# A first expert mixture over all tokens of nine experts against one over fifteen single-expert tiles of sent rows

## The reference, cut to what matters

```python
def _L0_ffn_ref(x, w_router, W1, b1, W2, b2, Ws1, bs1, Ws2, bs2):
    probs = jax.nn.softmax(jnp.einsum('btd,ed->bte', x, w_router), axis=-1)
    vals, idx = jax.lax.top_k(probs, TOP_K)                      # TOP_K = 2 of 8
    gates = jnp.sum(jax.nn.one_hot(idx, N_EXPERTS, dtype=x.dtype) * vals[..., None], axis=-2)
    hs = jax.nn.gelu(jnp.einsum('btd,fd->btf', x, Ws1) + bs1)    # shared expert
    acc = jnp.einsum('btf,df->btd', hs, Ws2) + bs2
    h = jax.nn.gelu(jnp.einsum('btd,efd->btef', x, W1) + b1)     # 128 -> 512
    y = jnp.einsum('btef,edf->bted', h, W2) + b2                 # 512 -> 128
    return SCALE * (acc + jnp.einsum('bted,bte->btd', y, gates))

def _L1_attn_ref(x, W_qkv, b_qkv, W_out, b_out, w_sur, b_sur, threshold):
    qkv = x @ W_qkv + b_qkv                                      # 16 heads of 8
    tq, sq = _expmap0_split(q); tk, sk = _expmap0_split(k)       # cosh and sinh of a norm
    dist = jnp.arccosh(jnp.maximum(tq tk - sq sk, 1.0 + 1e-07))
    attn = softmax(where(causal, -dist ** 2 / sqrt(D), -inf)) * spike_mask
...
x = x + _L0_ffn_ref(_layernorm(x), ...)
x = x + _L1_attn_ref(_layernorm(x), ...)
```

## Time and profile before

| | |
|---|---|
| median of three runs | 1193.46 us (1186.05, 1193.46, 1195.53) |
| the profiled execution's own time | 1186.87 us |
| its span | 1185.6 us |
| PE busy | 976.0 us, 82% of the span |
| DVE / ACT / POOL busy | 782.7 / 589.5 / 245.0 us |
| mean granted PE clock | 0.902 |
| bytes moved by DMA | 62.49 MB, mean 53 GB/s |
| on the chain that ended last | PE 57%, DVE 28%, ACT 5%, POOL 4% |

### The profile page before, as it was taken

How to read it: one execution, slowest core, us unless ns; L and a number is a source line. 1 busy time by engine, 2 the same in 40 slices (tenths; PEclk the granted TensorE clock), 3 DMA queues, 4 the chain that set the end, 5 groups by cost and what they waited for, 6 DMA issues and landing times.

```text
span 1185.6 us, 20975 instructions
## 1 busy us (share of the span) xinstructions
PE 976.0 (82%) x8169; PEld 552.0 (47%) x8169; DVE 782.7 (66%) x1990; ACT 589.5 (50%) x1019; POOL 245.0 (21%) x321
## 2 busy tenths in 40 slices
PE   6777779998999975767658999999578688689999
PEld 4233334444676752545433334566223233357667
DVE  7786888821326479878678963867787877664512
ACT  2556546674335347778627785223045456343342
POOL 2843220000000235967420000001120001100000
PEclk9898979998999985878877999999568889989999
DMA  8324250000000310491125007101003000100000
GB/s 315 103 71 94 63 188 2 3 5 1 1 1 1 107 37 1 143 182 54 47 68 185 2 3 107 43 1 44 11 28 134 2 1 2 36 1 1 10 1 10
DMA packets 35894, 62.49 MB, mean 53 GB/s; under 512 B 5235, under 2 KB 25668, under 8 KB 34196
## 3 DMA queue, kind: packets, MB, share of 16 engines
q1 hardware_dynamic: 33828, 58.64, 17.5%
q10 hardware_dynamic: 1968, 2.51, 0.8%
HBM read 43.04 MB, written 16.65 MB: 50 GB/s over the span
## 4 chain that ended last, share of the span: by engine, by line
PE 57%; DVE 28%; ACT 5%; POOL 4%; issue 3%; DMA 2%; SPq 1%; ACTq 0%; POOLq 0%; DVEq 0%
PE ps_s L970 10%; PE ps_e L960 10%; PE ps_v L759 7%; DVE mx L1999 6%; PE ps_e L649 4%; PE ps_e L1065 2%; DVE mx L1991 2%; PE ps_s L1052 2%; DVE ps_s L1973 2%; ACT work L1495 2%; PE ps_e L664 2%; DVE xn L1943 2%; PE ps_s L679 2%; DVE stats L1925 1%; DVE work L2532 1%
## 5 line engine op out<-in xcount | busy, mean ns | idle before, releaser
L1495 ACT ACTIVATE work<-ps_e 128x512 f32<-128x512 f32 x406 | 223.1, 597 | 110.5 <-PE ps_e L649 105.5
L2772 POOL TENSOR_TENSOR rstd<-rstd,halves 128x2 f32<-128x2 f32 x52 | 36.7, 706 | 657.4 <-DVE rstd L1930 657.0
L1999 DVE TENSOR_REDUCE mx<-ps_s 128x2 f32<-128x1024 f32 x128 | 153.6, 1221 | 21.0 <-PE ps_s L679 18.8
L1602 ACT ACTIVATE work<-ps_s,keep 128x512 f32<-128x512 f32 x136 | 93.0, 687 | 139.2 <-PE ps_s L970 136.1
L759 PE MATMUL ps_v<-work,vaug 128*32 128x256 f32 x1536 | 128.0, 408 | 5.0 <-ACT work L1483 4.9
L649 PE MATMUL ps_e<-q_stack,ctx_stack 52*128 52x256 bf16 (+1 forms) x684 | 121.7, 291 | 9.2 <-DMA q_stack<-mT 3.3
L960 PEld LDWEIGHTS ps_e<-ffn_w,work 128*128 128x128 f32 x960 | 117.2, 195 | 21.3 <-issue 19.6
L679 PE MATMUL ps_s<-ctx_stack,q_stack 49*128 49x512 bf16 (+1 forms) x296 | 91.6, 450 | 40.7 <-DVE mx L1999 30.7
L2198 DVE SCALAR_TENSOR_TENSOR x<-ps_e,gates,x 128x128 f32<-128x128 f32 x128 | 38.9, 346 | 124.8 <-PE ps_e L960 119.1
L970 PE MATMUL ps_s<-xnT,ffn_w 128*128 128x512 f32 x240 | 117.6, 614 | 3.6 <-ACT work L1602 3.6
L960 PE MATMUL ps_e<-ffn_w,work 128*128 128x128 f32 x960 | 119.3, 279 | 0.8 <-DVE x L2188 0.8
(11 more groups left out here) (412 smaller groups left out, 1965.9 us busy)
## 6 DMA issues: line engine op xcount, KB each, us to landing
q_stack<-q_scr SPq DMA_DIRECT2D x32, 192.0 KB
ffn_w<-in_L0f_w SPq DMA_DIRECT2D x1, 4608.0 KB, 17.5
ffn_w<-in_L1f_w SPq DMA_DIRECT2D x1, 3456.0 KB, 13.0
q_scr<-parts SPq DMA_DIRECT2D x16, 192.0 KB, 2.1
c_scr<-ffn_w SPq DMA_DIRECT2D x12, 256.0 KB, 7.6
kx_scr<-ffn_w SPq DMA_DIRECT2D x12, 256.0 KB, 3.9
ctx_stack<-kx_scr SPq DMA_DIRECT2D x2, 1536.0 KB
ctx_stack<-c_scr SPq DMA_DIRECT2D x2, 1536.0 KB
```

The costliest lines, as they stand in the source:

```text
L1495: act.activation(pt[:, parity, :, :].rearrange("p k q -> p (k q)"), bank[exp_bank(use, h, parity)], ACT.Exp).then_inc(exped, 1)
L1602: act.activation(hid_unit(st, u)[:, j, :], bank[f"h{n % 2}"], ACT.Gelu_apprx_tanh, bias=b1).then_inc(HIDS[st], 1)
L1999: m = dve.tensor_reduce(mx[:, b, :, pair, part], ps_s[i][:], AX, ALU.max, negate=True)
```

## The change

The mixture's eight routed experts run only over the rows that are sent to them.

- After the router of a half, DVE works out with a few small PE products (`rank`, `destinations`) at which row of a buffer each token's two copies go, so that every tile of 128 rows belongs to one expert, and which expert owns each of the `TILES` = 15 tiles.
- POOL sends the 1024 rows of a half by eight indirect DMAs to DRAM (`scatter`), SP brings the 15 tiles back in one transfer (`fetch_sent`, 960 KB), and PE transposes them (`turn_sent`).
- SP reads the 15 expert numbers into registers (`owners`) and fetches for every tile that expert's weights (128 x 1028 numbers, 514 KB) into a ring of `RING` = 4 places. The fetch for tile i waits until the down products of tile i-4 are done.
- PE does for each tile four up and four down products of 128 x 128 by 128 x 128, two tiles ahead with the ups. ACT does four GELUs of 128 x 128 for each and copies every four tiles' results out of PSUM. SP stores them, and POOL gathers each token's two rows back by eight indirect DMAs a half (`gather`). DVE adds them times the gates (`combine`).
- The shared expert stays dense. Of the products in the last slots of `X0` four are left where there were twelve.
- `EARLY_A1` = `TILES`, so all 36 steps of `l1_early` stand behind the last tile on PE and ACT, and on DVE ahead of `combine(2)` and `combine(3)`. On POOL `gather(1)` stands behind the splitting of batch 1.
- The single transfer of 4608 KB is gone.

```diff
+TILES = 2 * B * S // 2 // P + NE - 1
+RING = 4
+TILE_W = 2 * FH + FJ
+BLOCKS0 = -(-TILES // 4)
+UP_USE = {use: n for n, use in enumerate(
...
+RANK0 = 71
+RANK1 = 3
+GATES0 = 7
+EARLY_A1 = TILES
...
+        def turn_sent(g, q):
+            name = ("v", "m")[q % 2]
+            claim(name)
+            if q == 0:
+                pe.wait_ge(*after(x_there, 16 * (g + 1)))
+            for i in range(4 * q, min(4 * q + 4, TILES)):
+                m = pe.transpose(bank[name][:, i % 4 * P:(i % 4 + 1) * P], xg[:, i, :], ident)
+            m.then_inc(turned_x_ps[0], 1)
+            free[name] = after(turned_x, BLOCKS0 * g + q + 1)
+
...
+        def tile_up(g, i):
+            n, at = UP_USE["tile", g, i], g * TILES + i
+            name, w = f"h{n % 2}", tile_ring[at % RING]
+            claim(name)
+            pe.wait_ge(*after(tile_there[at % RING], 16 * (at // RING + 1)))
+            if i % 4 == 0:
+                pe.wait_ge(*after(turned_x, BLOCKS0 * g + i // 4 + 1))
+            for j in range(FJ):
+                m = pe.matmul(bank[name][:, j * P:(j + 1) * P], w[:, j * P:(j + 1) * P], xgT[:, i, :],
+                              start=True, stop=True)
+            m.then_inc(up_ps, 1)
+            free[name] = (hidden, n + 1)
+
+        def tile_down(g, i):
+            at = g * TILES + i
+            name, w, hid = f"e{i // 4 % 2}", tile_ring[at % RING], tile_hid[at % RING]
+            if i % 4 == 0:
+                claim(name)
+            pe.wait_ge(hidden, UP_USE["tile", g, i] + 1)
+            for j in range(FJ):
+                m = pe.matmul(bank[name][:, i % 4 * P:(i % 4 + 1) * P], hid[:, j, :], w[:, FH + j * E:FH + (j + 1) * E],
+                              start=(j == 0), stop=(j == FJ - 1))
+            m.then_inc(tile_ps[0], 1)
+            free[name] = after(evacuated, BLOCKS0 * g + i // 4 + 1)
+
...
+            shared_down(0)
+            shared_down(1)
+            for q in range(BLOCKS0):
+                turn_sent(0, q)
+            for g in range(2):
+                tile_up(g, 0)
+                tile_up(g, 1)
+                for i in range(TILES):
+                    if i + 2 < TILES:
+                        tile_up(g, i + 2)
+                    tile_down(g, i)
+                    if g == 0 and i == RANK1:
+                        rank(1)
+                    if g == 0 and i == GATES0:
+                        turn_gates("L0f", NE + 1, 1, ROUTE_AT["L0f"] + 1, "v")
+                        gated_bias("L0f", 0, NE + 1, 1, "m")
+                    if g == 1 and i >= EARLY_A1:
+                        l1_early(i - EARLY_A1)
+                if g == 0:
+                    for j in range(FJ):
+                        shared_up(1, j)
+                    for q in range(BLOCKS0):
+                        turn_sent(1, q)
+                    shared_down(2)
+                    shared_down(3)
+            for q in range(TILES - EARLY_A1, 36):
+                l1_early(q)
...
+        def tile_gelu(g, i):
+            n, at = UP_USE["tile", g, i], g * TILES + i
+            w, hid = tile_ring[at % RING], tile_hid[at % RING]
+            if at >= RING:
+                act.wait_ge(*after(tile_ps, at - RING + 1))
+            act.wait_ge(up_ps, n + 1)
+            for j in range(FJ):
+                m = act.activation(hid[:, j, :], bank[f"h{n % 2}"][:, j * P:(j + 1) * P], ACT.Gelu_apprx_tanh,
+                                   bias=w[:, 2 * FH + j:2 * FH + j + 1])
+            m.then_inc(hidden, 1)
+
+        def evacuate(g, k):
+            last = min(4 * k + 4, TILES)
+            n = (last - 4 * k) * P
+            if g == 1 and k == 0:
+                act.wait_ge(*after(y_stored, 16 * BLOCKS0))
+            act.wait_ge(*after(tile_ps, g * TILES + last))
+            act.activation(y_tile[:, k, 0:n], bank[f"e{k % 2}"][:, 0:n], ACT.Copy).then_inc(evacuated[0], 1)
 
...
+            for g in range(2):
+                tile_gelu(g, 0)
+                tile_gelu(g, 1)
+                for i in range(TILES):
+                    if i + 2 < TILES:
+                        tile_gelu(g, i + 2)
+                    if i % 4 == 3 or i == TILES - 1:
+                        evacuate(g, i // 4)
+                    if g == 1 and i >= EARLY_A1:
+                        l1_early(i - EARLY_A1)
+                if g == 0:
+                    for j in range(FJ):
+                        shared_gelu(1, j)
+            for q in range(TILES - EARLY_A1, 36):
+                l1_early(q)
...
+        def combine(b):
+            g = b // 2
+            dve.wait_ge(*after(y_gathered, 128 * (g + 1)))
+            dve.wait_ge(down_x, b + 1)
+            for c in range(2):
+                for t in tiles(b):
+                    m = dve.scalar_tensor_tensor(x[:, t, :], y_rows[:, g, c, t % 4, :], top_gates[:, c, t:t + 1],
+                                                 x[:, t, :], ALU.mult, ALU.add)
+                if c == 0:
+                    settle(m)
+            m.then_inc(combined[0], 1)
...
+            shared_add(0)
+            shared_add(1)
+            for q in range(BLOCKS0):
+                turned_sent(0, q)
+            route_rest("L0f", None, 1, slice(4, 8))
+            destinations(1, slice(4, 8))
+            turn_gates("L0f", NE + 1, 1, "v")
+            gated_bias("L0f", 1, "m")
+            for q in range(BLOCKS0):
+                turned_sent(1, q)
+            shared_add(2)
+            shared_add(3)
+            for b in (0, 1):
+                combine(b)
+                statistics(A1, b)
+                normalised(A1, b)
+            for q in range(36):
+                l1_early(q)
+            for b in (2, 3):
+                combine(b)
+                statistics(A1, b)
+                normalised(A1, b)
 
         def l3_piece(g, i):
             kind, e, k = PIECES[i]
...
+        def scatter(g):
+            pool.wait_ge(*after(destined, g + 1))
+            pool.wait_ge(*after(zeroed, 32))
+            if g == 1:
+                pool.wait_ge(*after(x_scattered, 128))
+            for t in range(4):
+                for c in range(2):
+                    pool.indirect_dma_start(
+                        out=x_sent[g][:, :],
+                        out_offset=bass.IndirectOffsetOnAxis(ap=dest_i[:, g, c * 4 + t:c * 4 + t + 1], axis=0),
+                        in_=xn[:, 4 * g + t, :], in_offset=None).then_inc(x_scattered[0], 16)
+
+        def gather(g):
+            pool.wait_ge(*after(y_stored, 16 * BLOCKS0 * (g + 1)))
+            if g == 1:
+                pool.wait_ge(*after(y_gathered, 128))
+            for t in range(4):
+                for c in range(2):
+                    pool.indirect_dma_start(
+                        out=y_rows[:, g, c, t, :], out_offset=None, in_=y_sent[g][:, :],
+                        in_offset=bass.IndirectOffsetOnAxis(ap=dest_i[:, g, c * 4 + t:c * 4 + t + 1], axis=0),
+                    ).then_inc(y_gathered[0], 16)
+
...
             split_keys(A1, 0, map_T, 2)
             split_keys(A1, 1, map_T, 4)
             split_queries(A1, 1, map_T, 3)
+            gather(1)
             l1_added_least(0)
...
-        for b in range(B):
+        for b in range(3):
             root("L0f", b)
+        scatter(0)
+        root("L0f", 3)
+        scatter(1)
+        gather(0)
         l1_attention()
...
+        def fetch_tile(g, i, owner):
+            at = g * TILES + i
+            if at >= RING:
+                sp.wait_ge(*after(tile_ps, at - RING + 1))
+            sp.dma_start(tile_ring[at % RING], d["L0f_tiles"][bass.ds(owner, 1)].rearrange("o p c -> (o p) c")) \
+                .then_inc(tile_there[at % RING][0], 16)
+
+        def owners(g):
+            sp.wait_ge(*after(destined, g + 1))
+            return [sp.value_load(expert_i[0:1, g, i:i + 1], min_val=0, max_val=NE - 1) for i in range(TILES)]
+
+        def fetch_sent(g):
+            sp.wait_ge(*after(x_scattered, 128 * (g + 1)))
+            if g == 1:
+                sp.wait_ge(*after(turned_x_ps, BLOCKS0))
+            sp.dma_start(xg, x_sent[g].rearrange("(i p) f -> p i f", p=P)).then_inc(x_there[0], 16)
+
+        def store_block(g, k):
+            n = min(4 * k + 4, TILES) - 4 * k
+            sp.wait_ge(*after(evacuated, BLOCKS0 * g + k + 1))
+            sp.dma_start(y_sent[g][4 * k * P:(4 * k + n) * P, :].rearrange("(i p) f -> p i f", p=P),
+                         y_tile[:, k, 0:n * P].rearrange("p (i f) -> p i f", i=n)).then_inc(y_stored[0], 16)
+
...
-        sp.dma_start(ffn_w[:, 0:FFN_N], d["L0f_w"][:, :]).then_inc(d_w, 16)
+        sp.dma_start(shared_w, d["L0f_shared"][:, :]).then_inc(d_w, 16)
+        for g in range(2):
+            sp.dma_start(x_sent[g][:, :], d["zeros"][:, :]).then_inc(zeroed[0], 16)
         for b in range(1, B):
             max_rows(X0, b)
+        owner = owners(0)
+        for i in range(RING):
+            fetch_tile(0, i, owner[i])
+        fetch_sent(0)
         sp.wait_ge(exp_ps, 2 * (STEP0[X0] + STEPS[X0]))
```

(19 more changed lines are left out.)

278 lines of the change are left out of this document (176 added, 102 removed).

## The result

The changed kernel takes 1230.28 us (median of 4 runs, 1226.28 to 1233.76) beside 1190.95 for the kernel before in the same session: 1.033 times, 95% interval 1.027 to 1.039. Run once more beside the experiments (e0_again) it gave 1225.19 us, 1.026 times (1.022 to 1.030). Forecast were 1208 and a range of 1188 to 1232. The sign was right; the loss is 39 us where 15 were forecast. The profiles of f1_banks and a4_again are of slower executions than the rest (over 1.5% above the fastest of the same kernel), so only lengths of stages are read from them.

The account below looks back on a forecast made before the run. PE was taken to bound the mixture. Batch 3 normalised at 450.5 against 434.6 gave +16 us, one us came back, +15; on the profiled 1186.9 that is 1202, plus 6.6 for the median 1208 us, range 1188 to 1232.

Parts of the forecast that it names:

- The end of X0: Before the mixture: eight ups removed bring the last batch's transposes some 5 us earlier; first down from 292.25 to 287.
- cover gone, it would cost these 4 us: End of X0: price of the 17 small DVE steps of destinations(0) if DVE were not waiting there.
- The work of the mixture: Shared expert and tiles: PE's 126 us become about 71, 1.78 us a tile; ACT and DVE don't set the pace.
- The ring of four sets the pace: Tile weights: a fetch takes 3.5 us, so two tiles take 5.3 us where PE needs 3.56; a half 38 us.
- First half: Tiles start at 293.5, half over at 333.5; indirect DMAs 1.3 us each, half 1's rows sent by 322, hidden.
- Between the halves: SP's queue: 15 reads of 0.6 us, then 12 us of transfers; second half's tiles start at 354.5, end at 392.5.
- The opening steps: Behind the last tile: 50.5 us to the last near product, 58 to batch 3 normalised, at 450.5 against 434.6.
- The gap did not close: Rival, between the halves: cheap register reads (0.1 us) close the gap, 14 us go, 1194 us; chance 0.20.
- the fetches were not hidden: Rival, tile weights: the fetches are hidden, 10 us go in each half, 1188 us; chance 0.05.
- the indirect DMAs were not 4 us: Rival, POOL's queue: indirect DMAs cost 4 us each, adding 5 us for sent rows and 14 at gather(1), 1227; chance 0.13.
- PE did not fall to its lower clock in the tiles: Rival, tiles: PE falls to 1.2 GHz, two tiles take 7.1 us instead of 5.3, 1239 us; chance 0.10.
- Faster: Whole kernel: faster by more than about 1%, under 1182 us, given 0.06; slower 0.57, same 0.37.

Follow-up runs that it names:

- f1_banks: Changed kernel with near products and roots of the opening steps taking two PSUM banks in turn instead of one: 1240.58 us, 1.036 times the kernel before.
- a4_again: Changed kernel with opening steps 0 to 20 between tiles 2 to 13 of the second half, second run: 1228.53 us, 1.023 times the kernel before.
- a1_again: Changed kernel with bank m freed early by a DVE copy of ranks and counts, second run: 1226.53 us, 1.026 times the kernel before.
- a3_once: Changed kernel fetching weights for the first four tiles only, later tiles reusing them (wrong experts): 1210.08 us, 1.011 times the kernel before.
- a5_ring6: Changed kernel with a ring of six places for tile weights instead of four: 1205.11 us, beside 1225.19 for the changed kernel.
- c2_serial: Changed kernel with ring of six, bank m freed early, sent rows and reads asked for earlier; opening steps still behind last tile: 1187.20 us, 0.991 times before.
- b1_serial: Kernel before, experts computed in full, with all 36 opening steps of A1 moved behind the mixture's last unit: 1234.22 us, 1.030 times before.
- a6_reads: Changed kernel, ring of four, half 1's sent rows asked for before tile 12's fetch, reads spread between fetches: 1226.43 us, 1.022 times the kernel before.
- a1_free_m: Changed kernel with bank m freed early by a DVE copy of ranks and counts, first run: 1238.37 us, 1.033 times the kernel before.
- a4_inter: Changed kernel with opening steps 0 to 20 between tiles 2 to 13 of the second half, first run: 1226.85 us, 1.022 times the kernel before.
- f2_best: Changed kernel with ring of six, bank m freed early, earlier sent rows and reads, two banks for near products: 1204.27 us, 1.008 times the kernel before.
- f3_best_late: The kernel of f2_best with opening steps 0 to 20 between tiles 9 to 14 of the second half: 1201.27 us, 1.005 times the kernel before.
- f3_again: The kernel of f3_best_late, unchanged, run once more: 1195.14 us, 1.001 times the kernel before.
- d1_again: Changed kernel with plain DMAs to and from fixed rows instead of POOL's 32 indirect ones (wrong rows), second run: 1234.28 us.

## Why the prediction was right or wrong

The forecast named the right places, and its sum was too small: +15 us, and 40 between the profiles. What failed is one wait that it did not have (the bank m, 5 us at the end of X0) and two terms that were too small: the fetch in the ring of four, put at 3.5 us with its wakes and measured at 4.1, and the twelve steps in one bank, put at 20.5 and measured at 24.9. Against the trace of the changed kernel, the 22.5 us between the forecast's 450.5 and the measured 473.0 for the normalised batch 3 are:

| step | forecast | measured | miss |
|---|---|---|---|
| tiles of half 0 start | 293.5 | 300.6 | 7.1 |
| half 0, with rank and gates | 40 | 45.4 | 5.4 |
| gap to the second half's tiles | 21 | 23.8 | 2.8 |
| half 1 | 38 | 41.3 | 3.3 |
| last tile to last near product | 50.5 | 54.7 | 4.2 |
| to the normalised batch 3 | 7.5 | 7.3 | -0.2 |

The other 2.6 of the 25 us lie behind it: the forecast had one us come back there, and 1.6 more were spent.

*The end of X0: failed.* The ups taken out do give 4 us: from batch 2's root to batch 3's it is 22.9 us instead of 26.8. But I hid `destinations(0)` "in a place where DVE is waiting" and looked only at DVE. The bank m, which PE claims next, is free only with DVE's last small step: PE stood 2.3 us, came back at the lower of its two clocks (granted 0.50 from 254 to 258), and lost 5 us: 32.3 us from batch 1's root to batch 2's, where the kernel before has 27.3. The price "cover gone, it would cost these 4 us" was nearly right. a1_again shows it by removing it: 27.4 us between the roots. Of the other 2 us of the 7.1, one is that the ups taken out give 4 and not 5; the last one I can't place.

*The work of the mixture: right in kind.* GELUs of 128 columns take 0.37 us, four of them 1.15 us (I had 1.2). PE's pair is 2.04 us per fetch, not 1.78, as the first product behind a wait starts slower (1.13 us for eight records against 0.89).

*The ring of four sets the pace: right, shown by a3_once and a5_ring6; its term was too small.* The landing on the chain is 3.4 to 4.5 us, not 3.2, with 0.14 us on either side; a pair 6.15 on average, not 5.3. Two rows a factor of five apart in size were joined by a line, and the larger one had the queue to itself; here other fetches are in flight beside each. That this makes them longer fits the 4.9 us with a ring of six, and was not tried by itself. My upper bound of 4.9 held it, and with 4.1 in place of 3.5 and 2.04 for 1.78 the same sum gives 6.15.

*First half: sent rows in time, right.* Indirect DMAs are 0.96 us, 1.26 us from start to start (forecast 1.3); the rows of half 1 are sent by 328 instead of 322, needed at 351. All of them are hidden. Beside the longer fetches, PE was at its lower clock for two stretches of some 3 us (eight records in 1.7 us instead of 0.89, at 309.9 and 330.5).

*Between the halves: right to 3 us.* Reads 0.58 us (forecast 0.6); by the Trainium skill, "DMA: Bandwidth & Descriptors", Latency and other measured facts, a `tensor_load` has a floor of about 600 ns, and the trace agrees. The 960 KB landed 13.4 us after the first fetch was asked for at 347.9 (forecast 12). c2_serial shows that the gap is SP's queue and not PE.

*The opening steps: mechanism right, one term mis-sized.* 29.7 us from the last tile to the first near product (forecast 28). The twelve steps in one bank took 24.9 where I had 20.5, with 1.7 us each from rows of a PE at its upper clock; at the lower one the first piece of a product takes 0.50 instead of 0.34 us, and DVE's squares of the roots, 1.36 and 2.97 us, which my twelve equal steps left out, stand between. I added "2 for a PE that is mostly idle" and needed 4 more. b1_serial settles that this placing alone costs 40 us where the mixture is computed in full.

*Rivals.* The gap did not close, the fetches were not hidden, the indirect DMAs were not 4 us. PE did not fall to its lower clock in the tiles as a whole (granted 0.91 and 1.00). The Trainium skill, "TensorE: Matmul & The Clock Gate", HAM oscillation, tells of a kernel whose clock falls in each wait for operands of 3 to 5 us between short bursts. In the second half of the changed kernel PE's waits are of 0.3 to 2.0 us only, as part of each fetch of 4 us lies under products, and the clock stays at 1.00; behind the one wait of 3.9 us in a6_reads it was 0.50, which agrees with the page. Nor did DVE's work slow POOL's indirect DMAs: the eight of the last gather start 1.26 us apart (439.6 to 448.4) under DVE's reductions and squares, as those at 263 with DVE mostly idle; whether a copy in a two-port mode would, no run shows. The one wait that no term or rival had was a bank held over a DVE sequence. "Faster" was rightly small.

The better kernel follows from the same list: with the ring of six, the free bank and SP's queue in another order the tiles end at 370, 41 us earlier than in the changed kernel, and the 62 us behind them then end where the kernel before had them: 1187 us, 0.9% under it where PE does not stand still. Counted from batch 1's root to the last norm that kernel is 3 us shorter than the one before (200.5 against 203.5); the other 5 us between the medians lie outside this stage and were not traced.

## What to carry to other kernels

Work that is cheap because it lies in the shadow of a busy engine can come to the full price when that shadow is made shorter: before counting what a sparse stage spares, list what it was covering, and move that only to where it has another cover and its inputs are there. In this ring the latency of one fetch under the load of the others set the depth that was needed, not the queue's rate. When a step is hidden "in idle time of an engine", ask also which buffer it holds meanwhile and who claims that next.

## What the hardware showed that I had not expected

On three of the six chips or sessions used, the kernels with indirect DMAs had PE standing still for 1.5 to 5 us at three to five places while or just after POOL's indirect DMAs ran (eight profiles: a1_free_m, a3_once, a4_inter, f1_banks, a4_again, f2_best, f3_best_late, f3_again); behind them the granted clock was 0.50 for up to 12 us, and the stretch from batch 2's root to batch 3's took 29.8 to 32.3 us instead of 22.9. In the other sessions none of eight such profiles had one. b1_serial, without indirect DMAs, and d1_again, with plain ones, ran in sessions of the first kind and had none. That points to the indirect DMAs, but by two profiles only. A rival that was not tried is the loading of PE's code: a transfer of the instruction queue lies near the first of these places, yet it does so in the profiles without a standstill too (the changed kernel, e0_again, d1_again, b1_serial). Why only some sessions have them stays open. It is a reason to compare such kernels only with runs made beside them; the changed kernel itself ran only in two sessions without standstills, and gave 1.033 and 1.026 there.
